# Finding the tokens of an expert's tile: scattered rows and a sorted table, or a sorted order inverted by one-hot products and gathered rows

## The chip, the core and the metric

One core of one Trainium2 chip runs the kernel. The metric is the device time of one execution in microseconds. Engines: TensorE (PE), VectorE (DVE), ScalarE (ACT), GpSimd (POOL), SyncE (SP); 16 transfer engines move data between the core's SBUF and HBM. PSUM holds what TensorE writes.

## The reference

`x` is 4 x 1024 tokens of 256 numbers, normalised per token to `xn`. The result is the sum of three things:

```python
xn = _layernorm(x, axis=-1)
x = x + attention(xn, Wq, Wk, Wv) + experts(xn, w_gate, w_in, w_out)

# experts: 8 experts, each token goes to its two best
logits = xt @ w_gate.T
top_logits, top_idx = jax.lax.top_k(logits, 2)
gates = (one_hot(top_idx, 8) * softmax(top_logits)[..., None]).sum(axis=1)
for e in range(8):
    y = y + gates[:, e:e+1] * ((xt @ w_in[e].T) @ w_out[e].T)
```

The attention has 16 heads by 4 batches, 64 independent problems of 1024 positions with 16 features each (the heads are cut out of the projections by a plain reshape), followed by a normalisation over each batch.

## The kernel before

The tokens are taken as 32 tiles of 128 (`NT`), in 8 chunks of 4 tiles (`NC`, `TC`).

**Products and projections** (to about 224 us). For each expert, `w_in` and `w_out` are multiplied into one 256 x 256 matrix (`mm`). VectorE and GpSimd normalise each chunk into `xn`. TensorE transposes a chunk (`transposes`, L1006), projects values and gate logits (`project_v`, L1033: four groups of six products a chunk) and queries and keys (`project_qk`, L1018: four outputs of six products). ScalarE reads each output of `project_qk` out of PSUM (L580), VectorE subtracts to get the low half (L710), SyncE stores both (L336). Outputs 2 and 3 wait until outputs 0 and 1 have been read by both, since two PSUM banks are shared.

**The plan of the sorted order**, on VectorE, for each half of the tokens (`PARTS` = 2, 16 tiles each): `choose_experts` and `count_choices` every second chunk; TensorE's `rank_choices` turns counts into ranks; `start_tiles` finds how many tiles of 128 rows each expert gets and where they start; `place_choices` gives each token and choice its row number `placeu` in the sorted order (row 128 * tile + row in tile); `place_padding` finds rows for the ends of tiles; `name_owners` (L805 to L812) packs the expert of each of the 40 tiles (`TILES`) into words that TensorE reads. For part 0 this stands in chunk 4, for part 1 after chunk 7.

**The sorted table.** When a part is placed, GpSimd issues 32 indirect transfers (L462), each of which scatters one tile's 128 rows of `xn` to their places in the DRAM table `xs_d`, once for each choice, and then 8 more (L468) that write zero rows into the padding.

**The experts** (about 284 to 381 us). 80 sorted tiles are worked in 20 blocks of 4. SyncE's `sorted_tokens` (L390) loads a block from `xs_d` into one of two halves of `xnc`; TensorE transposes it, ScalarE and VectorE split it into `xth` and `xtl`, `expert_tile` (L1117) multiplies each tile by its expert's matrix, ScalarE and VectorE add the halves, and SyncE's `expert_rows` (L394) stores the block to `ys_d`. From block 4 on, each block also carries one step of attention maxima (`max_scores`, `maxima`). The four output buffers are used in turn, so ScalarE waits at block 4 for the store of block 0.

**The attention loop** (from about 381 us) goes over 64 heads by batches, two ahead with the maxima. In every second round GpSimd gathers a token tile's two expert rows from `ys_d` (L480, two indirect transfers) and weighs and adds them.

SyncE's queue is in order. Its part around the change, after the last stores of `project_qk`: `regroup` 0 to 7 (L323), the loads `features` of the first four rounds (L355) after a wait for `att_const` >= 2, `values(0)` (L360), and only then the expert blocks. `att_const` counts the constant fills of `kf` (GpSimd, L450, ones) and `ot`. The queue's lines around the first block:

```python
for n in range(SLOTS):
    sp.wait_ge(regrouped[n % BC], 16 * (n // BC + 1))
    features(n)
sp.wait_ge(v_stored, 16 * NC)
values(0)
...
sp.wait_ge(m_ready, KT * E)
sorted_tokens(0)
sorted_tokens(1)
```

## Time and profile before

| | us |
|---|---|
| median of three runs | 1091.26 |
| lowest, highest | 1086.12, 1094.1 |
| the profiled execution, its own time | 1090.37 |
| its span, first to last instruction | 1087.7 |

| engine | busy in the span |
|---|---|
| TensorE | 85% |
| VectorE | 75% |
| ScalarE | 62% |
| GpSimd | 26% |

A row of a timeline reads: start in us, duration in us, engine, line of the kernel, instruction, what it writes <- what it reads, count, and in brackets how long the engine stood idle before it and what ended that. PE rows show when products start; their ends are modelled. A row of the chain of waits is a start, a duration and what held the end back at that time; "issue" is time in which nothing was waited for that the profile shows. For an indirect transfer the duration is GpSimd's own work, not the movement of data.

### The profile page before, as it was taken

The page shows a single profiled execution, that of the slowest core. Times are in us where ns is not written, and L with a number is a line of the kernel's source. Part 1 is how long each engine was busy: PE and PEld are TensorE (multiplying, and loading weights), DVE is VectorE, ACT ScalarE, POOL GpSimd, SP SyncE. Part 2 cuts the span into 40 slices and gives each one's busy share as a digit, 9 for nine tenths or more (in the row PEclk, how much of TensorE's full clock was granted, in tenths as well). Part 3 has the DMA queues.
Part 4 walks back from the last instruction along what each step waited for, and adds up shares of the span by engine and source line. Part 5 has one row for each costly group of instructions (what it writes and reads, how often), then busy time and mean ns, then how long its engine had stood idle before and what let it go on. Part 6 is the DMA issues. An engine that isn't in the chain of part 4 may idle for free.

```text
span 1087.7 us, 20730 instructions
## 1 busy us (share of the span) xinstructions
PE 926.8 (85%) x7540; PEld 464.2 (43%) x7540; DVE 821.0 (75%) x1106; ACT 678.4 (62%) x1347; POOL 283.5 (26%) x450
## 2 busy tenths in 40 slices
PE   7886852520499999999999999999999999999994
PEld 6765741520387733333333333333333333333332
DVE  4452540350188779999999999999999999989976
ACT  2210420210165568888888888888888888878884
POOL 2000057127400013232222223232323232223230
PEclk9997986665599979999999999999999999999998
DMA  8675475376587524333333433343334333333214
GB/s 290 236 278 194 149 221 158 112 228 199 159 265 231 175 70 112 100 100 98 105 101 97 103 103 103 93 110 100 103 90 112 100 98 100 105 98 90 73 45 155
DMA packets 155075, 148.44 MB, mean 136 GB/s; under 512 B 84064, under 2 KB 125792, under 8 KB 154976
## 3 DMA queue, kind: packets, MB, share of 16 engines
q1 hardware_dynamic: 148064, 128.24, 40.0%
q0 software_dynamic: 6912, 18.88, 5.6%
q8 instruction: 61, 1.00, 0.4%
q14 instruction: 38, 0.31, 0.1%
HBM read 99.62 MB, written 63.18 MB: 150 GB/s over the span
## 4 chain that ended last, share of the span: by engine, by line
PE 69%; DMA 13%; SPq 5%; issue 4%; DVE 3%; another core or an unknown queue 3%; ACT 2%; POOL 0%; ACTq 0%; POOLq 0%; DVEq 0%
PE ps L1166 21%; PE ps L1148 19%; DMA qf<-ot 10%; PE ps L1136 8%; PE ps L1117 6%; PE ps L1045 5%; PE ps L1018 3%; PE ps L1006 2%; PE ps L1033 2%; SPq L355 2%; DMA wp<-w_out_t 1%; SPq L370 1%; PE ps L1189 1%; DMA xnc<-xs_d 1%
## 5 line engine op out<-in xcount | busy, mean ns | idle before, releaser
L826 DVE TENSOR_REDUCE negm<-ps 128x1 f32<-128x1024 f32 x512 | 619.9, 1223 | 42.4 <-PE ps L1136 22.9
L630 ACT ACTIVATE wp<-ps 128x512 f32<-128x512 f32 x684 | 369.8, 602 | 64.2 <-PE ps L1148 44.3
L1148 PE MATMUL ps<-qf,kf 50*128 50x512 f32 x1024 | 390.3, 456 | 9.1 <-DMA qf<-ot 7.1
L1136 PE MATMUL ps<-kf,qf 48*128 48x512 f32 x1024 | 365.9, 449 | 0.8 <-DVE negm L826 0.7
L1148 PEld LDWEIGHTS ps<-qf,kf 50*128 50x128 f32 x1024 | 162.1, 186 | 216.1 <-ACT wp L630 99.7
L1166 PE MATMUL ps<-wp,vb 128*17 128x256 f32 x2736 | 215.8, 387 | 0.1
L1136 PEld LDWEIGHTS ps<-kf,qf 48*128 48x128 f32 x1024 | 146.9, 186 | 6.0 <-issue 5.0
L630 ACT ACTIVATE vstage<-ps 128x512 f32<-128x512 f32 x170 | 102.3, 602 | 31.5 <-PE ps L1148 21.2
L501 POOL TENSOR_TENSOR mpart<-negm,zero 128x8 fp32r<-128x8 f32 x64 | 13.1, 205 | 397.0 <-DVE negm L826 397.0
L630 ACT ACTIVATE picks<-ps 128x512 f32<-128x512 f32 x170 | 102.4, 602 | 0.0
L1166 PEld LDWEIGHTS ps<-wp,vb 128*17 128x17 f32 x2736 | 46.9, 95 | 116.7 <-issue 40.5
L462 POOL DMA_INDIRECT xs_d<-xn,placeu x64 | 62.3, 973 | 90.9 <-DVE placeu L786 72.0
L695 DVE TENSOR_TENSOR xtl<-ps,xth 128x512 fp32r<-128x512 f32 x56 | 36.4, 687 | 63.7 <-issue 53.0
L555 ACT CAST xth<-ps 128x512 fp32r<-128x512 f32 x56 | 30.5, 590 | 66.4 <-issue 56.9
L508 POOL TENSOR_TENSOR xn<-xn,odd 128x256 f32<-128x256 f32 x32 | 23.5, 733 | 172.7 <-DVE odd L843 172.7
L1006 PE MATMUL ps<-ident,xnc 128*128 128x128 f32 x160 | 23.3, 294 | 52.5 <-issue 52.5
L480 POOL DMA_INDIRECT xnc<-ys_d,placeu x64 | 62.1, 971 | 15.5 <-issue 10.5
L1117 PE MATMUL ps<-mm,xth 128*128 x160 | 61.9, 433 | 4.6 <-issue 4.5
L1045 PE MATMUL ps<-wp 128*128 128x256 f32 x176 | 45.9, 422 | 19.9 <-DMA wp<-w_out_t 18.9
L710 DVE TENSOR_TENSOR spare<-ps,stage 128x512 f32<-128x512 f32 x20 | 13.8, 692 | 58.0 <-issue 30.1
L1166 PE MATMUL ps<-vstage,vb 128*17 128x256 f32 x680 | 53.6, 387 | 0.2 <-issue 0.2
L1166 PE MATMUL ps<-picks,vb 128*17 128x256 f32 x680 | 53.2, 385 | 0.0
(171 smaller groups left out, 895.2 us busy)
## 6 DMA issues: line engine op xcount, KB each, us to landing
feat_d<-qk_d SPq DMA_DIRECT2D x64, 256.0 KB, 3.5
qf<-feat_d SPq DMA_DIRECT2D x128, 128.0 KB
xnc<-xs_d SPq DMA_DIRECT2D x20, 512.0 KB
qf<-feat_d SPq DMA_DIRECT2D x128, 64.0 KB
kf<-feat_d SPq DMA_DIRECT2D x128, 64.0 KB
qk_d<-wp SPq DMA_DIRECT2D x24, 256.0 KB
wp<-w_in SPq DMA_DIRECT2D x11, 512.0 KB, 5.1
wp<-w_out_t SPq DMA_DIRECT2D x11, 512.0 KB, 6.5
```

Source lines behind the costliest of these rows:

```text
L462: nc.gpsimd.indirect_dma_start(out=xs_d[part], out_offset=bass.IndirectOffsetOnAxis(ap=placeu[:, k, t:t + 1], axis=0), in_=xn[:, t, :], in ...
L480: nc.gpsimd.indirect_dma_start(out=xnc[:, t % 2, k, :], out_offset=None, in_=ys_d[part], in_offset=bass.IndirectOffsetOnAxis(ap=placeu[:, ...
L630: nc.scalar.activation(weight_tile(n, j, b)[:, h * HALF:(h + 1) * HALF], ps[:, ST_BANK[(2 * unit + b) % 3], :], ACT.Exp).then_inc(exp_done, 1)
L695: nc.vector.tensor_tensor(xtl[:, p, kt, :], ps[:, XT_BANK[kt], :], xth[:, p, kt, :].bitcast(FP32), ALU.subtract).then_inc(xtl_done, 1)
L826: nc.vector.tensor_reduce(negm[:, n % 2, qt:qt + 1], ps[:, b:b + 2, :].rearrange("p b c -> p (b c)"), AX.X, ALU.max, negate=True).then_inc ...
L1006: last = nc.tensor.transpose(ps[:, XT_BANK[kt], t * P:(t + 1) * P], tokens[:, kt * P:(kt + 1) * P], ident[:])
L1018: last = nc.tensor.matmul(ps[:, PROJECT_BANK[o % 2], :], w[:, o // 2, kt, (o % 2) * P:(o % 2 + 1) * P], v[:, p, kt, :], start=i == 0, stop ...
L1045: last = nc.tensor.matmul(ps[:, M_BANK[dh], 0:D], win[slot][:, h, dh * P:(dh + 1) * P], wout[slot][:, h, :], start=s == 0 and h == 0, stop ...
L1117: last = nc.tensor.matmul(ps[:, Y_BANK[i % 4], 0:columns], v[:, p, kt, tokens], m[:, kt, bass.ds(e * (2 * D), columns)], start=j == 0, sto ...
L1136: last = nc.tensor.matmul(ps[:, max_bank(turn) + half, :], qf[rows, u, qt * P:(qt + 1) * P], kf[rows, u, :], start=True, stop=True)
L1148: nc.tensor.matmul(ps[:, ST_BANK[(2 * unit + half) % 3], :], kf[rows, u, j * P:(j + 1) * P], qf[rows, u, h * HALF:(h + 1) * HALF], start=T ...
L1166: last = nc.tensor.matmul(ps[32 * c:32 * c + VW, PV_BANK, 0:POS // 4], vb[:, n % 2, j + b * NKT // 2, :], weight_tile(n, j, b)[:, c * (POS ...
```

## The change

The sorted table and the scatters go. SyncE stores the normalised tokens plainly into `xn_d` (`tokens_out`, one store of 0.5 MB a chunk: four ahead of the stores of chunk 2, then one behind the stores of each of chunks 2 to 5). VectorE and TensorE invert the sorted order: for each of a part's 32 pairs of token tile and choice, `row_hot` holds a one where the row number in the tile equals the column, `tile_hot` the token's number where the tile equals the column, and 32 products added up in one PSUM bank give, for each row of each of the 40 tiles, which token belongs there; padding rows give token 0. `take_sources` copies that to `source`. GpSimd then gathers each sorted tile from `xn_d` straight into `xnc`, 80 gathers in all, and from the third block on waits until TensorE has transposed the block that was in the buffer. The one-hots lie in `qf` and `kf`, so `kf` is filled with ones only afterwards, by VectorE; SyncE's `features` wait for that. `place_padding` goes. In part 0, `find_sources` stands at the head of chunk 5 and `take_sources` at the head of chunk 6; on TensorE the 32 products stand between the transposes of chunk 6 and `project_qk` of chunk 5.

```diff
+            def tokens_out(c):
+                part, first = c * PARTS // NC, c * CH % (PT * P)
+                sp.wait_ge(xn_done, TC * (c + 1))
+                sp.dma_start(xn_d[part][first:first + CH].rearrange("(t p) d -> p t d", p=P), xn[:, TC * c:TC * (c + 1), :]
+                             ).then_inc(xn_out[part], 16)
...
+            for c in range(NC // PARTS):
+                tokens_out(c)
             for c in range(2, NC):
                 values_out(c)
                 qk_halves_out(c)
+                if c + 2 < NC:
+                    tokens_out(c + 2)
...
-            sp.wait_ge(m_ready, KT * E)
-            sorted_tokens(0)
-            sorted_tokens(1)
             for b in range(NMB):
-                if b + 2 < NMB:
-                    sorted_tokens(b + 2)
...
-            nc.gpsimd.memset(kf[:].bitcast(FP32), 1.0).then_inc(att_const, 1)
...
-            for part in range(PARTS):
-                for k in range(2):
-                    pool.wait_ge(placed, 2 * part + k + 1)
-                    for t in range(PT * part, PT * (part + 1)):
-                        nc.gpsimd.indirect_dma_start(
-                            out=xs_d[part], out_offset=bass.IndirectOffsetOnAxis(ap=placeu[:, k, t:t + 1], axis=0),
-                            in_=xn[:, t, :], in_offset=None).then_inc(scattered[part], 16)
-                pool.wait_ge(att_const, 2)
-                pool.wait_ge(padded, part + 1)
-                for e in range(E):
-                    nc.gpsimd.indirect_dma_start(
...
+            for part in range(PARTS):
+                pool.wait_ge(sourced, part + 1)
+                pool.wait_ge(named, part + 1)
+                pool.wait_ge(xn_out[part], 16 * NC // PARTS)
+                for i in range(TILES):
+                    b = part * MB + i // TC
+                    if i % TC == 0 and b >= 2:
+                        pool.wait_ge(xt_psum, KT * (NC + b - 1))
+                    nc.gpsimd.indirect_dma_start(
+                        out=xnc[:, b % 2, i % TC, :], out_offset=None, in_=xn_d[part],
+                        in_offset=bass.IndirectOffsetOnAxis(ap=source[:, part, i:i + 1], axis=0)).then_inc(xs_in[b % 2], 16)
+                    if b == WARM + NKT + 3 and i % TC == TC - 1:
+                        max_halves(0)
...
+            def find_sources(part):
+                count, tiles, base, place, placef, owner, packed, work, row, tile, split = plans[part]
+                rows = slice(PT * part, PT * (part + 1))
+                parts = split.bitcast(mybir.dt.uint32).rearrange("p (h k t) -> p h k t", h=2, k=2)
+                for half, (op, number, out) in enumerate(((ALU.bitwise_and, P - 1, row), (ALU.logical_shift_right, 7, tile))):
+                    g(nc.vector.tensor_scalar(parts[:, half], placeu[:, :, rows], number, None, op))
+                    g(nc.vector.tensor_copy(out, parts[:, half].rearrange("p k t -> p (k t)")))
+                g(nc.vector.tensor_tensor(tile_hot, iota[:, 0:TILES].unsqueeze(1).to_broadcast([P, 2 * PT, TILES]),
+                                          tile.unsqueeze(2).to_broadcast([P, 2 * PT, TILES]), ALU.is_equal))
+                for k in range(2):
+                    own = tile_hot[:, k * PT:(k + 1) * PT]
+                    g(nc.vector.tensor_tensor(own, own.bitcast(FP32), token[:].unsqueeze(2).to_broadcast([P, PT, TILES]), ALU.mult))
+                for k in range(2):
+                    own = slice(k * PT, (k + 1) * PT)
+                    nc.vector.tensor_tensor(row_hot[:, own], iota[:].unsqueeze(1).to_broadcast([P, PT, P]),
+                                            row[:, own].unsqueeze(2).to_broadcast([P, PT, P]), ALU.is_equal).then_inc(hot, 1)
+                dve.wait_ge(hot, 2 * (part + 1))
+
+            def take_sources(part):
+                dve.wait_ge(found, part + 1)
+                nc.vector.tensor_copy(source[:, part], ps[:, RANK_BANK[part], 0:TILES]).then_inc(sourced, 1)
...
-            place_padding(1)
+            find_sources(1)
             name_owners(1)
+            take_sources(1)
+            nc.vector.memset(kf[:].bitcast(FP32), 1.0).then_inc(att_const, 1)
...
+            def find_sources(part):
+                for k in range(2):
+                    pe.wait_ge(hot, 2 * part + k + 1)
+                    for t in range(k * PT, (k + 1) * PT):
+                        last = nc.tensor.matmul(ps[:, RANK_BANK[part], 0:TILES], row_hot[:, t].bitcast(FP32),
+                                                tile_hot[:, t].bitcast(FP32), start=t == 0, stop=t == 2 * PT - 1)
+                last.then_inc(found, 1)
```

## Rows read from the trace of the kernel before

**Rows 1.** Busy time by stage: stretch, its length, busy us of each engine, clock, DMA, GB/s.
```profile
150.00:202.00 52.00, 10.86 (x33) 7.13 (x31) 4.13 (x8) 4.30 (x10) 33.70 (x35) 0.63 0.54 161
202.00:224.10 22.10, 21.04 (x98) 17.27 (x98) 10.74 (x34) 8.49 (x24) 0.00 (x0) 0.87 0.50 162
224.10:284.30 60.20, 1.66 (x7) 1.40 (x7) 12.23 (x59) 0.79 (x2) 36.78 (x38) 0.53 0.69 210
284.30:380.60 96.30, 89.99 (x513) 73.48 (x513) 72.86 (x135) 51.00 (x119) 2.33 (x4) 0.92 0.66 207
380.60:1060.00 679.40, 669.18 (x6175) 258.51 (x6175) 629.77 (x599) 562.73 (x1068) 188.99 (x317) 0.99 0.36 96
```

**Rows 2.** Timeline of ScalarE, chunk 5: it reads outputs of `project_qk`.
```profile
172.43 0.59 ACT L580 CAST stage<-ps 128x512 fp32r<-128x512 f32 x1 [9.51 <-remote]
189.42 0.59 ACT L580 CAST stage<-ps 128x512 fp32r<-128x512 f32 x1 [16.41 <-issue]
200.90 0.59 ACT L580 CAST stage<-ps 128x512 fp32r<-128x512 f32 x1 [10.89 <-remote]
```

**Rows 3.** Timeline of TensorE, chunk 5: first and last products of the third output.
```profile
163.79 1.22 PE L1018 MATMUL ps<-xth,wqkh 128*128 128x512 f32 x2 [9.26 <-issue]
...
165.67 1.05 PE L1018 MATMUL ps<-xth,wqkl 128*128 128x512 f32 x2
```

**Rows 4.** Timeline of GpSimd: a fill; first and last transfers of part 0; last of part 1.
```profile
3.03 1.80 POOL L450 MEMSET kf<- 128x2048 f32 x1
...
143.41 1.25 POOL L462 DMA_INDIRECT xs_d<-xn,placeu  x1 [30.18 <-DVE placeu L786]
...
193.32 0.96 POOL L468 DMA_INDIRECT xs_d<-ot,padu  x1 [0.31 <-issue]
...
285.73 0.96 POOL L468 DMA_INDIRECT xs_d<-ot,padu  x1 [0.30 <-issue]
```

**Rows 5.** Chain of waits, from the first feature load to the first expert transposes.
```profile
243.69 1.15 SPq L355
...
270.09 12.71 DMA xnc<-xs_d
...
284.29 1.94 PE ps L1006 x8
```

**Rows 6.** Chain of waits in the projections and in the experts.
```profile
149.40 0.87 PE ps L1006 x8
...
202.26 4.33 PE ps L1033 x18
...
221.03 3.08 PE ps L1018 x12
...
308.49 0.87 PE ps L1006 x8
...
374.19 0.87 PE ps L1006 x8
```

**Rows 7.** Timeline of VectorE: end of part 0's planning; part 1's last placing, padding, first owner step.
```profile
150.05 0.17 DVE L812 CAST words<-xnc 128x5 int32<-128x5 f32 x1
...
236.50 0.17 DVE L786 TENSOR_SCALAR placeu<-wp 128x16 uint32<-128x16 f32 x1
...
238.25 0.23 DVE L799 TENSOR_SCALAR padu<-wp,lane 128x8 uint32<-128x8 f32 x1
238.52 0.45 DVE L805 TENSOR_TENSOR wp<-iota,wp 128x280 f32<-128x280 f32 x1
```

**Rows 8.** Timelines: ScalarE with and without a gather pair just before; GpSimd's last gather.
```profile
497.40 0.60 ACT L630 ACTIVATE vstage<-ps 128x512 f32<-128x512 f32 x1 [0.33 <-PE ps L1148]
...
506.29 0.60 ACT L630 ACTIVATE vstage<-ps 128x512 f32<-128x512 f32 x1 [0.23 <-PE ps L1148]
...
1054.31 0.95 POOL L480 DMA_INDIRECT xnc<-ys_d,placeu  x1 [0.30 <-issue]
1057.12 1.04 POOL L487 TENSOR_TENSOR xnc<-xnc,gates 128x512 f32<-128x512 f32 x1 [1.86 <-DMA xnc<-ys_d,placeu]
```

More of the change, by code:

```diff
@@ L62, in attention_and_experts @@
     v_d = nc.dram_tensor("v_d", [T, 2, NKT * VW], FP32, kind="Internal").ap()
-    xs_d = [nc.dram_tensor(f"xs_d{i}", [TILES * P, D], FP32, kind="Internal").ap() for i in range(PARTS)]
+    xn_d = [nc.dram_tensor(f"xn_d{i}", [PT * P, D], FP32, kind="Internal").ap() for i in range(PARTS)]
     ys_d = [nc.dram_tensor(f"ys_d{i}", [TILES * P, D], FP32, kind="Internal").ap() for i in range(PARTS)]
@@ L118, in attention_and_experts @@
         before = sb("before", [P, PT + 1, E])
-        padu = sb("padu", [P, PARTS, E], mybir.dt.uint32)
+        source = sb("source", [P, PARTS, TILES], mybir.dt.uint32)
         placeu = sb("placeu", [P, 2, NT], mybir.dt.uint32)
         words = sb("words", [P, PARTS, WORDS], mybir.dt.int32)
-        odd = sb("odd", [P, D])
+        odd = lg[:].rearrange("p t e -> p (t e)")
         wp = sb("wp", [P, 4, POS])
@@ L208, in attention_and_experts @@
         placed = sem("placed")
-        padded = sem("padded")
+        hot = sem("hot")
+        sourced = sem("sourced")
+        found = sem("found")
         named = sem("named")
-        scattered = sem("scattered", PARTS)
+        xn_out = sem("xn_out", PARTS)
         xs_in = sem("xs_in", 2)
@@ L759, in start_tiles @@
             def start_tiles(part):
-                count, tiles, base, place, placef, owner, packed, work, filled, excess, inside = plans[part]
+                count, tiles, base, place, placef, owner, packed, work, row, tile, split = plans[part]
                 bank = RANK_BANK[part]
@@ L770, in start_tiles @@
                                           iota[:, 0:MOST].unsqueeze(1).to_broadcast([P, E, MOST]), ALU.is_gt))
-                g(nc.vector.reduce_sum(tiles[:, :, 0], more, AX.X))
-                g(nc.vector.tensor_tensor(tiles[:, :, 1], tiles[:, :, 0], count, ALU.subtract))
-                g(nc.vector.memset(base[:, 0], 0.0))
-                for e in range(E):
-                    g(nc.vector.tensor_tensor(base[:, e + 1], base[:, e], tiles[:, e], ALU.add))
+                g(nc.vector.reduce_sum(tiles, more, AX.X))
+                g(nc.vector.memset(base[:, 0:1], 0.0))
+                for e in range(1, E):
+                    g(nc.vector.tensor_tensor(base[:, e:e + 1], base[:, e - 1:e], tiles[:, e - 1:e], ALU.add))
                 g(nc.vector.tensor_tensor(place, ps[:, bank, 0:PT * E].rearrange("p (t e) -> p t e", e=E),
-                                          base[:, 0:E, 0].unsqueeze(1).to_broadcast([P, PT, E]), ALU.add))
+                                          base.unsqueeze(1).to_broadcast([P, PT, E]), ALU.add))
             def place_choices(part):
-                count, tiles, base, place, placef, owner, packed, work, filled, excess, inside = plans[part]
+                count, tiles, base, place, placef, owner, packed, work, row, tile, split = plans[part]
                 rows = slice(PT * part, PT * (part + 1))
@@ L787, in place_choices @@
                     dve.wait_ge(placed, 2 * part + k + 1)
[L789 to L800 removed]
+            def find_sources(part):
+                count, tiles, base, place, placef, owner, packed, work, row, tile, split = plans[part]
+                rows = slice(PT * part, PT * (part + 1))
[13 more added lines that the diff above has]
+                dve.wait_ge(hot, 2 * (part + 1))
@@ L802, in name_owners @@
+            def take_sources(part):
+                dve.wait_ge(found, part + 1)
+                nc.vector.tensor_copy(source[:, part], ps[:, RANK_BANK[part], 0:TILES]).then_inc(sourced, 1)
             def name_owners(part):
-                count, tiles, base, place, placef, owner, packed, work, filled, excess, inside = plans[part]
+                count, tiles, base, place, placef, owner, packed, work, row, tile, split = plans[part]
                 past = work[:, 0:TILES * (E - 1)].rearrange("p (i e) -> p i e", e=E - 1)
-                g(nc.vector.tensor_tensor(past, iota[:].unsqueeze(2).to_broadcast([P, TILES, E - 1]),
-                                          base[:, 1:E, 0].unsqueeze(1).to_broadcast([P, TILES, E - 1]), ALU.is_ge))
+                g(nc.vector.tensor_tensor(past, iota[:, 0:TILES].unsqueeze(2).to_broadcast([P, TILES, E - 1]),
+                                          base[:, 1:E].unsqueeze(1).to_broadcast([P, TILES, E - 1]), ALU.is_ge))
@@ L884, in _ @@
                 planned = c == NC // PARTS
+                if c == NC // PARTS + 1:
+                    find_sources(0)
+                if c == NC // PARTS + 2:
+                    take_sources(0)
                 if c % PAIR == 0 and c > PAIR:
@@ L1096, in _ @@
                     rank_choices(0)
+                if c == NC // PARTS + 1:
+                    find_sources(0)
                 for o in range(4):
@@ L1099, in _ @@
             rank_choices(1)
+            find_sources(1)
             def owner_words(part):
```

51 lines of the change are left out of this document (16 added, 35 removed).

## Prediction

> **What bounds the kernel now.** I read four views in this order: the busy time by stage, the chain of waits, the timelines of each engine where the chain breaks off, and the groups of operations for prices. By stage [rows 1], 679 of 1087.7 us are the attention loop (from 380.6), in which TensorE, VectorE and ScalarE are all nearly full. The change leaves that loop alone, so whatever it gives or takes lies before 380.6. There two stages are nearly empty: from 150 to 202 TensorE is busy 10.9 of 52 us, and from 224.1 to 284.3 it is busy 1.7 of 60 us. VectorE and ScalarE are empty there as well, while GpSimd issues indirect transfers in both.
>
> The second gap is plain in the chain [rows 5]. SyncE issues the loads of the attention features from 243.7 on. Only after them, at 270.1, comes the load of the first sorted block. It lands 12.7 us later, and TensorE starts on the experts at 284.3. Even a faster load could not help much: the last of the scatters that must land before the first load of part 1, and that share the transfer engines, is issued at 285.7 [rows 4].
>
> The first gap is odd. ScalarE reads the second, third and fourth result of `project_qk` of chunk 5 at 172.4, 189.4 and 200.9 [rows 2], after waits of 9.5, 16.4 and 10.9 us. TensorE's six products that the read at 189.4 takes are shown from 163.8 to 166.7 [rows 3]. Nothing else stands between. So a result of TensorE reaches its reader some 20 us late. This begins about 6 us after the first scatter is issued and ends at 200.9; GpSimd issues the 40 scatters of part 0 from 143.4 to 194.3 [rows 4]. Afterwards the same work flows: the last three value groups of chunk 6 start at 202.3, and all is done at 224.1 [rows 6]. I read the gap as the price of the scatter stream. From 149.4 to 202.3 TensorE gets through one set of transposes (0.9), four outputs of `project_qk` (two take 3.1, so 6.2) and one value group (about 1.0) [rows 6]: 8.1 us of work in 52.9. The rest, 44.8 us over 40 scatters, is 1.12 us for each.
>
> **What the change removes.** All 80 scatters (two parts of 32 and 8), the 20 sorted loads from SyncE's queue, eight padding steps per part on VectorE (1.8 us, from the end of the placing to that of the padding [rows 7]), and two small steps of planning (0.4). The constant fill of `kf` leaves GpSimd (1.8 [rows 4]) where it was hidden.
>
> **What it adds, stage by stage.**
>
> *Chunk 5.* `find_sources(0)` stands at the head of chunk 5 on VectorE, ahead of all that TensorE waits for. Steps of 16 and 280 elements take 0.17 and 0.45 [rows 7], so 1.06 ns for each further element. Four small steps cost 0.7, the tile one-hot of 1280 elements 1.5, two products of 640 together 1.7, two row one-hots of 2048 2 x 2.32 = 4.6, and nine gaps of 0.03 0.3: 8.8 us. VectorE ended its planning at 150.2 [rows 7]; without padding it ends at 148.4, and with the new work at 157.2. TensorE then has 16 of its 32 small products left. A transpose with the same 128-column weight costs 0.109 at the 2.4 GHz clock (granted 1.0) and 0.243 at 1.2 GHz [rows 5, 6], so 1.7 to 3.9; I take 2.8. Chunk 5's `project_qk` starts at 160.0 and takes 6.2. Chunks 6 and 7 take 22.8, from 201.3 (202.3 less the first value group) to 224.1. TensorE ends the projections at 189.0, before at 224.1. The new stores of 0.5 MB a chunk lie beside it: the transfer engines were at half load from 202 to 224 [rows 1]. If they did bind, four chunks of 0.52 MB at the full rate (162 GB/s at half load, so 324) would be 6.5 us. I take nothing.
>
> *Between projections and experts.* In the old kernel the second placing ended at 236.7 [rows 7], 12.6 after 224.1; 12.2 without the two steps. Add 8.8 for `find_sources(1)`, 3.9 for the last 16 products at the low clock of this stretch (0.53 [rows 1]), 0.2 for `take_sources`, 1.8 for the fill of `kf`, bounded by GpSimd's row. `name_owners` hides under the products. Sum 26.9, where the old kernel took 60.2. The fill holds up `features` on SyncE, and behind them `values(0)` and `expert_rows`. Features and values took 26 us [rows 5], so the first block's rows leave at about S + 26, S being the start of the experts. ScalarE needs that slot again only at block 4, at S + 24 by the old pace (308.5 less 284.3 [rows 5, 6]). I take nothing; it could be some 5 us, once.
>
> *Experts.* Blocks 0 and 1 are fetched long before. The other 18 need 72 gathers at 1.28 each (39 steps from 143.4 to 193.3 [rows 4]): 92.2. GpSimd may start on block 2 once the first transposes are done (1.9), the last block lands 1.9 after its issue (1055.3 to 1057.1 [rows 8]), and from the last transposes at 374.2 to the end it is 6.4 [rows 1, 6]. The chain by GpSimd is 102.4, TensorE's own 96.3 [rows 1], hence 6.1 slower.
>
> *The unknown.* What does a gather cost TensorE? I call it s. 8 gathers lie in the projections and 72 in the experts, so the experts end at the later of 318.3 + 8s (GpSimd) and 189.0 + 26.9 + 96.3 + 80s = 312.2 + 80s (TensorE). The upper bound is the scatter's 1.12. The lower is 0, a transfer that takes nothing from TensorE; that it would help is excluded. In between lies the one mark that I find, a wait of ScalarE for TensorE of 0.33 in the step after the pair, 0.23 in the like step without gathers [rows 8]. The nearest row is the gather's own, though it shows pairs and no stream. I put the whole 0.33 on a pair, s = 0.17. Then the experts end at 325.8 instead of 380.6, 54.8 earlier. The span becomes 1032.9, and with the 2.7 around it **1036 us**. The profiled run (1090.4) is 0.9 below the median of three, which changes nothing here.
>
> The Trainium skill speaks against my reading of the first gap. "SBUF — State Buffer", section "Who interferes with whom", says that the DMA side and the engine side are disjoint and that "PE and ACT never wait on anyone". By it the late results are not the scatters' doing. This case's rows show the coincidence and not the mechanism, so it is carried as a rival.
>
> **The rivals.**
>
> *A stream of gathers costs like a stream of scatters* (s = 1.12). For it: both come from the same queue at the same pace, and a pair may be too short to build up what 40 in a row did. Against it: the old kernel's first eight transposes for the experts, at 284.3, show 1.9 us, the plain low-clock time, although 78 scatters had been issued by then [rows 4, 5]. Experts' end 312.2 + 89.6 = 401.8, time 1112. The gain is gone from s = 0.86 on. Chance 0.17, of which 0.02 within 1%.
>
> *In between* (s from 0.3 to 0.85): 1046 to 1090, middle 1066. Chance 0.20, 0.03 of it within 1%.
>
> *The late results have another cause and stay.* The projections then end at 224.1 + 9.8 (planning until 160.0 instead of 150.2) = 233.9, the experts at 233.9 + 26.9 + 102.4 = 363.2, time 1073. That is the time by the skill's sentence above. Against it speaks that the standstill begins and ends with the scatters. Chance 0.10.
>
> *Faster still*, below 1020, if GpSimd gets ahead or the small products cost less: 0.05.
>
> **How the numbers follow.** The likeliest case (s below 0.3, 1028 to 1046) has 0.48, and 1036 is its value at s = 0.17; with the stores binding it would reach 1052. The range must take in the middle and the third rival, so 1020 to 1090. Outside are 0.05 below and 0.15 above. A measurement of this kernel tells about 1% from no change. Faster by more: 0.48 + 0.17 + 0.10 + 0.05 = 0.80. Within 1%: 0.05. Slower: 0.15.
>
> **What would show it.** Chunk 5's four reads by ScalarE about 1.5 us apart, and the projections' end near 190: the first gap was the scatters'. VectorE's six large steps together 7.7, TensorE's 32 small products within 8. First expert transposes near 217. Then GpSimd without pause at 1.28 a gather, and blocks of experts about 5.1 us apart. If the blocks are 6 or more apart, with TensorE's results read late, the rivals with the larger s are right. If GpSimd waits for transposes between blocks, the landing time is what I have too small. The attention loop should keep its 679 us; a change there I have not foreseen.

## The result and the profile after

The changed kernel takes 1073.3 us (median of 4 runs) against 1091.7 for the kernel before on the same chip: a ratio of 0.984, 95% interval 0.980 to 0.988. On another chip, in a later group of runs, it was 0.989 (0.985 to 0.994). The forecast was 1036. So the change makes the kernel faster, by 1.6% and a third of what I expected. The profiled execution took 1073.4 us with a span of 1071.4, beside the forecast span of 1032.9: 38.5 us are missing.

Busy time by stretch, changed kernel: the rest of the projections, the gap to the experts, the experts, and all that follows. Columns: stretch, its length, busy time of TensorE, its weight loads, VectorE, ScalarE and GpSimd with instructions, granted clock, share of the transfer engines, GB/s.

```profile
145.00:202.50 57.50, 45.68 (x225) 38.63 (x224) 25.61 (x59) 14.30 (x42) 7.81 (x8) 0.85 0.54 179
202.50:237.50 35.00, 15.54 (x71) 15.13 (x71) 20.67 (x60) 0.79 (x2) 0.00 (x0) 0.57 0.48 128
237.50:374.80 137.30, 102.43 (x513) 80.76 (x513) 74.34 (x138) 49.54 (x120) 68.47 (x74) 0.84 0.57 160
374.80:1071.40 696.60, 681.71 (x6311) 262.16 (x6311) 646.01 (x626) 577.36 (x1092) 191.04 (x320) 0.98 0.37 100
```

The same two last stretches of the kernel before, cut at the same marks (first expert transposes, first attention product):

```profile
284.30:382.10 97.80, 90.44 (x513) 73.63 (x514) 73.92 (x138) 51.37 (x120) 2.33 (x4) 0.92 0.65 204
382.10:1087.70 705.60, 682.79 (x6311) 264.42 (x6311) 646.22 (x626) 576.36 (x1092) 191.69 (x320) 0.98 0.37 99
```

Both gaps of [rows 1] have shrunk, as forecast: the projections end at 202.5 us instead of 224.1, and the experts start 35 us later instead of 60. But the expert stage takes 137.3 us instead of 97.8, 39.5 more. I had allowed it some 14 more. And the attention loop with its tail, which the change does not touch, is 9.0 us shorter.

Timeline of ScalarE, changed kernel, the four reads of chunk 5's `project_qk`; and later waits for TensorE in chunk 6, then one for a store:

```profile
170.33 0.59 ACT L579 CAST stage<-ps 128x512 fp32r<-128x512 f32 x1 [15.89 <-PE ps L1030]
171.65 0.59 ACT L579 CAST stage<-ps 128x512 fp32r<-128x512 f32 x1 [0.73 <-PE ps L1030]
173.49 0.58 ACT L579 CAST stage<-ps 128x512 fp32r<-128x512 f32 x1 [1.25 <-PE ps L1030]
174.89 0.59 ACT L579 CAST stage<-ps 128x512 fp32r<-128x512 f32 x1 [0.81 <-PE ps L1030]
...
185.87 0.58 ACT L579 CAST wp<-ps 128x512 fp32r<-128x512 f32 x1 [2.52 <-remote]
188.72 1.07 ACT L579 CAST wp<-ps 128x512 fp32r<-128x512 f32 x2 [2.27 <-remote]
194.14 0.17 ACT L563 COPY lg<-ps 128x8 f32<-128x8 f32 x1 [4.34 <-DMA v_d<-vstage]
```

("remote" is a wait whose end the profile can't put to any instruction.) The reads that waited 9.5, 16.4 and 10.9 us in [rows 2] now wait 1.3 us at most. What delays them is the 15.9 us ahead of the first: the planning. The chain of waits shows how that time is made up, for part 0 and then part 1, with the store that binds in between:

```profile
149.36 1.50 DVE kf L794
150.89 0.84 DVE kf L798
...
152.61 2.30 DVE qf L801
154.96 12.66 PE ps L1105 x64
...
181.78 12.29 DMA v_d<-vstage
...
218.78 2.30 DVE qf L801
221.12 13.89 PE ps L1105 x64
```

VectorE's steps have the sizes that I gave them (1.50, 0.84, 2.30). The 32 small products do not: they are 64 records, in 12.7 us.

In the experts three kinds of waits appear. GpSimd's timeline at the head of blocks; ScalarE's; one start of TensorE's transposes; and two pieces of the chain of waits:

```profile
252.18 0.94 POOL L504 DMA_INDIRECT xnc<-xn_d,source  x1 [2.54 <-PE ps L1018]
...
258.40 0.94 POOL L504 DMA_INDIRECT xnc<-xn_d,source  x1 [1.54 <-PE ps L1018]
...
284.49 0.94 POOL L504 DMA_INDIRECT xnc<-xn_d,source  x1 [9.49 <-PE ps L1018]
```

```profile
251.71 0.92 ACT L610 COPY spare<-ps 128x256 f32<-128x256 f32 x3 [2.51 <-remote]
...
278.35 0.37 ACT L610 COPY spare<-ps 128x256 f32<-128x256 f32 x1 [10.95 <-DMA ys_d<-spare]
...
300.50 0.37 ACT L610 COPY stage<-ps 128x256 f32<-128x256 f32 x1 [3.18 <-remote]
```

```profile
268.94 1.10 PE L1018 MATMUL ps<-ident,xnc 128*128 128x128 f32 x8 [1.25 <-DMA xnc<-xn_d,source]
```

```profile
262.23 16.10 DMA ys_d<-spare
...
294.24 5.53 DMA xnc<-xn_d,source
```

GpSimd is not the unbroken chain that I assumed. It waits 1.1 to 4.5 us for TensorE's transposes at 12 of the 18 blocks that it gathers in the stage, and 9.5 us at one more; between the long waits a block takes about 6 us instead of 5.1. ScalarE waits 2.5 to 3.2 us for some results: the products that the read at 300.50 takes had ended at 297.7. At block 4 everything stands for some 10 us, until the first expert rows, whose store is issued at 262.23, have landed in `ys_d` at 278.33. And the gathers land later than the 1.9 us of the forecast: the block whose transposes start at 268.94 had its last gather issued at 262.15, 6.8 us before, and the chain has another with 5.5. With two buffers, GpSimd gets through without a wait only if the block has landed and is transposed within about 6.2 us of its last issue (five gathers of 1.25), so a landing time like this alone makes it wait.

### The profile page after: what moved, and what is told of

Same layout as the page of the kernel before. It is cut to its first block, busy times and chain, and to the rows that moved or that the text cites. A ratio compares the mean times of both kernels' runs of the same rounds, so it can differ in the third digit from the quotient of the medians.

```text
span 1071.4 us, 20973 instructions
## 1 busy us (share of the span) xinstructions
PE 960.4 (90%) x7668; PEld 493.0 (46%) x7668; DVE 836.1 (78%) x1107; ACT 677.3 (63%) x1347; POOL 279.2 (26%) x448
## 3 DMA queue, kind: packets, MB, share of 16 engines
q1 hardware_dynamic: 141728, 121.95, 38.5%
## 4 chain that ended last, share of the span: by engine, by line
PE 73%; DMA 9%; DVE 6%; SPq 5%; issue 3%; ACT 1%; POOL 1%; POOLq 0%; ACTq 0%; DVEq 0%
PE ps L1189 25%; PE ps L1171 21%; PE ps L1159 10%; PE ps L1057 4%; DMA qf<-ot 3%; PE ps L1030 2%; PE ps L1140 2%; DMA v_d<-vstage 2%; PE ps L1105 2%; SPq L364 2%; SPq L345 2%; DMA ys_d<-spare 2%; PE ps L1018 1%; DMA wp<-w_out_t 1%; PE ps L1200 1%
## 5 line engine op out<-in xcount | busy, mean ns | idle before, releaser
L504 POOL DMA_INDIRECT xnc<-xn_d,source x80 | 75.9, 948 | 169.4 <-PE ps L1018 82.7
L629 ACT ACTIVATE vstage<-ps 128x512 f32<-128x512 f32 x170 | 102.4, 602 | 27.6 <-PE ps L1171 16.5
L1140 PE MATMUL ps<-mm,xth 128*128 x160 | 67.6, 463 | 21.1 <-DVE spare L824 13.3
L492 POOL TENSOR_TENSOR xn<-xn,lg 128x256 f32<-128x256 f32 x32 | 23.4, 731 | 172.7 <-DVE lg L850 172.6
L694 DVE TENSOR_TENSOR xtl<-ps,xth 128x512 fp32r<-128x512 f32 x56 | 37.1, 687 | 19.4 <-ACT xth L554 12.7
L1057 PEld LDWEIGHTS ps<-wp 128*128 128x128 f32 x176 | 37.2, 215 | 26.6 <-issue 11.3
L641 ACT COPY ot<-ps 128x384 f32<-128x384 f32 (+1 forms) x64 | 30.4, 476 | 22.5 <-PE ps L1212 20.5
```

The lines of the kernel that those rows point to most:

```text
L504: nc.gpsimd.indirect_dma_start(out=xnc[:, b % 2, i % TC, :], out_offset=None, in_=xn_d[part], in_offset=bass.IndirectOffsetOnAxis(ap=sourc ...
L629: nc.scalar.activation(weight_tile(n, j, b)[:, h * HALF:(h + 1) * HALF], ps[:, ST_BANK[(2 * unit + b) % 3], :], ACT.Exp).then_inc(exp_done, 1)
L641: nc.scalar.copy(ot[:, 0:groups, n % 2, :], ps[:, PV_BANK, 0:groups * TB].rearrange("p (g t) -> p g t", t=TB)).then_inc(pv_evac, 1)
L694: nc.vector.tensor_tensor(xtl[:, p, kt, :], ps[:, XT_BANK[kt], :], xth[:, p, kt, :].bitcast(FP32), ALU.subtract).then_inc(xtl_done, 1)
L1057: last = nc.tensor.matmul(ps[:, M_BANK[dh], 0:D], win[slot][:, h, dh * P:(dh + 1) * P], wout[slot][:, h, :], start=s == 0 and h == 0, stop ...
L1140: last = nc.tensor.matmul(ps[:, Y_BANK[i % 4], 0:columns], v[:, p, kt, tokens], m[:, kt, bass.ds(e * (2 * D), columns)], start=j == 0, sto ...
```

## The experiments

All ratios are to the kernel before on the same chip. A run is called by the first part of its label (e5, b3). "Stage" is the expert stage, from its first transposes to the first attention product.

**The small products.** The changed kernel with

```diff
-  nc.tensor.matmul(..., row_hot[:, t].bitcast(FP32), tile_hot[:, t].bitcast(FP32), ...)
+  nc.tensor.matmul(..., row_hot[:, t], tile_hot[:, t], ...)
```

> The changed kernel with the 64 small products that find the source tokens read as FP32R instead of FP32, nothing else. In the changed kernel they are 64 records in 12.7 us at 155 us and 64 records in 13.9 us at 221 us, two for each product of about 0.2 us. Theory A (the two passes of an FP32 product are what my estimate left out, and both places lie on the path that sets the end): 32 records of 0.2 us, 6.3 and 7 us less, the span 11 to 13 us shorter. Theory B (chunk 5's end is set by the stores that the vstage buffer waits for, so the first place gives nothing): 7 us less, all of it between 215 and 237 us. Theory C (the one-hots' weight loads or VectorE's one-hots are the bound): no change.

Chain of waits of this kernel, the same two places:

```profile
156.09 2.30 DVE qf L801
158.43 7.01 PE ps L1105 x32
...
217.76 7.03 PE ps L1105 x32
```

32 records in 7.0 us at both places, 5.7 and 6.9 less. The time is 1063.6 us, ratio 0.976 (0.969 to 0.982). The products gave what theory A says. The projections ended only 3.4 us earlier (199.7 by the end of their last read, for 203.1), since the products of part 0 also started 3.5 us later in this execution (158.4 for 155.0, behind VectorE's one-hots); in part 1 nothing took the gain away. One product is 0.22 us in FP32R and 0.40 in FP32, both at a granted clock of 0.50 to 0.55. In the forecast I had priced it by a transpose (0.109 to 0.243), which is FP32 too but is recorded once.

**The features ahead of the stores.** The changed kernel with SyncE's list reordered:

```diff
-  for n in range(SLOTS): features(n)
-  values(0)
   for b in range(NMB):
+      if b < SLOTS: features(b)
+      if b == SLOTS: values(0)
       if b: expert_rows(b - 1)
```

> The changed kernel with SyncE's list changed: the four feature blocks and the first values are issued one at a time between the first stores of expert outputs, instead of all ahead of the first store. Theory A (the stall at the expert stage's block 4, 9.5 us of GpSimd's and 10.9 us of ScalarE's waiting for ys_d<-spare, comes from the store behind the features on SyncE): the stall is gone, the expert stage 139 us becomes 128 to 131, the time 8 to 11 us shorter. Theory B (the store itself is slow because the DMA engines are full with the features' transfers, 16.1 us for 0.5 MB, and would be in any order): under 3 us.

ScalarE has no wait for `ys_d` left in the stage, and the stage takes 130.0 us, 7.4 less. The time is 1066.4, ratio 0.978 (0.971 to 0.986). So the stall at block 4 was the queue, as theory A has it. The prediction had named it ("some 5 us, once") and put it at nothing. For e1 and e2 alike the gain is read from the stretches: the intervals of their ratios overlap that of the changed kernel (0.980 to 0.988), so that the whole times don't show it by themselves.

**No gathers.** The changed kernel with 20 plain loads in place of the 80 gathers:

```diff
-  nc.gpsimd.indirect_dma_start(out=xnc[:, b % 2, i % TC, :], in_=xn_d[part], in_offset=source...)
+  sp.dma_start(xnc[:, b % 2], xn_d[b // MB][first:first + CH]...)
```

> The changed kernel with the 80 gathers of the expert stage replaced by 20 plain loads of the same bytes from the same table, issued by SyncE two blocks ahead as in the kernel before; the search for the sources stays, its result is not used, so that the rows reach the experts unsorted (this part of the computation is left out). Theory A (the gathers make the stage 139 us instead of 96: GpSimd's pace, their latency and TensorE's late results while they are generated): the stage takes 97 to 108 us, the time 30 to 40 us shorter, and no ScalarE read waits over 1.5 us for a TensorE result in it. Theory B (features and stores in the DMA queues are what lengthened it): 120 us or more.

1054.8 us, ratio 0.965 (0.959 to 0.972), and a stage of 116.9 us, 20.4 less than the changed kernel's: between the two theories. The chain of waits tells why:

```profile
255.76 12.98 DMA xnc<-xn_d
268.78 1.97 PE ps L1026 x8
...
282.83 2.09 PE ps L1148 x12
...
300.04 2.11 PE ps L1148 x12
```

The load of block 2 stands behind the features on SyncE and costs about 20 us at the start. Afterwards a block takes 4.3 us (from 282.83 to 300.04 are four), and no read of ScalarE is late. TensorE's own pace is thus 4.3 us, and the changed kernel's 6 are the gathers' doing (late results and late landings together; this run takes both away). The store and feature traffic is a second, separate cause, which shows as soon as the first is gone.

**What the scatters did.** The kernel before with part 0's 40 scatters held back:

```diff
   for part in range(PARTS):
       for k in range(2):
-          pool.wait_ge(placed, 2 * part + k + 1)
+          pool.wait_ge(placed, 2 * PARTS)
```

> The kernel before, with the 40 scatters of part 0 held back until part 1 is placed, so that none is issued during chunk 5 of the projections; all is still computed. Theory A (the stream of scatters made TensorE's results late, 1.12 us each over 40): chunk 5 has no ScalarE read that waits over 2 us, the projections end at 196 to 202 us instead of 224; afterwards 80 scatters in a row take 102 us from about 197, so that the experts start 15 to 35 us later relative to the projections' end and get late results themselves: the time 1090 to 1130. Theory B (the late results have another cause, such as the stores of q and k halves): the projections still end at 218 or later.

The projections end at 186.5 us instead of 224.7 (last read ended), the chunk-5 reads follow each other as in the changed kernel. The standstill has moved to where the scatters now are, from 198.8 to 300 us. Timeline of ScalarE there:

```profile
275.49 0.58 ACT L555 CAST xth<-ps 128x512 fp32r<-128x512 f32 x1 [10.80 <-remote]
286.63 0.58 ACT L555 CAST xth<-ps 128x512 fp32r<-128x512 f32 x1 [10.56 <-remote]
297.83 0.37 ACT L611 COPY spare<-ps 128x256 f32<-128x256 f32 x1 [10.61 <-remote]
```

One result comes through every 11 us, which is about nine scatters. The time is 1107.5, ratio 1.012. Whoever moves the scatters moves the standstill with them: that they cause it is shown. 38.2 us over 40 scatters are 0.96 us each, stores that they slow included (see e8 below); my reading of [rows 2 to 4] had 1.12.

**Scatter or gather, bytes or count, stream or single.** Three variants of the kernel before. The first pauses the stream, the other two keep the real scatters back as above and put 32 small transfers (128 rows of 128 bytes) in their place:

```diff
+  if part == 0 and t % 4 == 3:
+      pool.wait_ge(scattered[part], 16 * (k * PT + t + 1))
```

```diff
+  nc.gpsimd.indirect_dma_start(out=<idle xnc>, in_=x as rows of 32, in_offset=placeu...)      # e6
+  nc.gpsimd.indirect_dma_start(out=small_d, out_offset=placeu..., in_=xn[:, t, 0:32])         # e7
```

> The kernel before, with GpSimd waiting, after every fourth token scatter of part 0, until those already issued have landed; all is computed. With the scatters held back until later chunk 5 had no late result and the projections ended at 186.5 us instead of 224.7. Theory A (what delays TensorE's results is an unbroken run of indirect transfers, and a pause lets them through): the reads of chunk 5 wait at most 5 to 6 us each (four scatters) instead of 8.3 to 15, the projections end at 195 to 205 us, the time 0 to 25 us shorter (the stream takes eight waits of some 2 us longer). Theory B (each scatter costs TensorE its 1.12 us, paused or not): the projections still end at 220 or later.

> The kernel before with part 0's 40 scatters held back until part 1 is placed, as in e4_late_scatters, and in their old place, from 149 us, 32 gathers of 128 rows of 128 bytes each (from the input into an idle buffer; extra work, the rest is all computed). Theory A (any unbroken run of indirect transfers holds TensorE's results, gathers too): reads of chunk 5 wait 8 us and more, the projections end at 210 to 225 instead of 186.5. Theory B (only scatters do it): the projections end at 186 to 190.

> As e6_small_gathers, with 32 scatters of 128 rows of 128 bytes (into a table of their own) in place of the 32 gathers. Theory A (it is the generating of the transfers, not their 1 KB rows, that holds TensorE's results): the projections end at 210 to 225, as with 1 KB rows. Theory B (bytes in the DMA engines or in SBUF's read path): 186 to 195.

And one to see whether the place of the buffers changes the attention loop, with `odd = lg[:]...` as in the changed kernel:

> The kernel before with the attention rows of a pair kept in the idle logits buffer instead of a buffer of their own, as the changed kernel does; this moves every buffer behind it by 1 KB per partition. The 29 rounds of the attention loop took 622.5 and 623.8 us in the two kernels with the old buffers and 614.5 to 616.9 in the four with the new ones, the difference in waits for the maxima's rows (qf<-ot). Theory A (it comes from where the buffers lie): 614 to 618 us, the time 6 to 9 us shorter. Theory B (it comes from the phase in which the loop is entered, or from the tables in HBM): 621 to 625 us, the time the same within 3 us.

None of these four says what it was sent to say. e5 ended its projections at 197.6 us, e6 at 194.6, e7 at 194.3; but e8, which issues exactly the old 40 scatters in a row, ended them at 206.6, and its reads are not late at all. Timeline of ScalarE in e8:

```profile
155.90 0.59 ACT L580 CAST stage<-ps 128x512 fp32r<-128x512 f32 x1 [1.26 <-PE ps L1018]
157.31 0.59 ACT L580 CAST stage<-ps 128x512 fp32r<-128x512 f32 x1 [0.82 <-PE ps L1018]
171.49 0.17 ACT L564 COPY lg<-ps 128x8 f32<-128x8 f32 x1 [13.60 <-DMA v_d<-vstage]
```

In this group the scatters only slow a store (13.6 us of waiting for `v_d`). TensorE's results are in time. The kernel before was itself faster here, 1080.2 us against 1093.1 in the first group. Either the chip of this group did not show the effect, or the moved buffers took it away (e8 has them; in e5 to e7 the scatters were paused or replaced). The ratios were 0.989 (0.985 to 0.993) for e5 and 0.998 (0.995 to 1.002) for e8; e6 and e7 ran once each, at 1072.8 and 1071.9 us.

The same three kernels went to another chip, beside a profile of the kernel before and of the changed one on a third:

> The kernel before, unchanged, profiled on the chip of this group. In the second group of runs no kernel showed a late TensorE result, though one of them (e8_att_in_lg) issued the same 40 scatters in a row; in the first group and in the two profiles shown at the start they came up to 24 us late. Theory A (the delay belongs to some chips and not to others): either late results as in the first profile (projections' end 220 to 228 us) or none (204 to 210), and the other three kernels of this group alike. Theory B (it was the 1 KB shift of the buffers in e8_att_in_lg and the held-back scatters in the others that took it away): projections' end 220 to 228 us here on any chip.

> The changed kernel, unchanged, on the same chip. Theory A: if the kernel before shows no late results here, neither does this one, and the expert stage is 8 to 12 us shorter than the 137 us of its first profile, the stall at block 4 kept; the ratio to the kernel before stays between 0.975 and 0.99. If it shows them, the profile is as the first.

> The same kernel as e8_att_in_lg, on another chip. Theory A (late TensorE results belong to some chips; three groups showed them, one did not): with late results the projections end at 218 to 228 us, without them at 204 to 208, and the three kernels beside it agree. Theory B (the 1 KB shift of the buffers took them away): 204 to 208 here though the others of the group show them.

> The same kernel as e6_small_gathers: the kernel before with part 0's scatters held back and 32 gathers of 128 rows of 128 bytes from 149 us on. If this chip shows late results at all: Theory A (any unbroken run of indirect transfers holds TensorE's results, gathers as scatters): reads of chunk 5 that wait 4 to 16 us, the projections' end at 205 to 222. Theory B (gathers do far less): 186 to 197.

> The same kernel as e5_scatter_pauses: a wait for landing after every fourth scatter of part 0. If this chip shows late results at all: Theory A (a pause lets them through): no read of chunk 5 waits over 6 us, the projections end at 190 to 205. Theory B (each transfer costs its 1.12 us, paused or not): 218 or later.

The kernel before again ended its projections at 223.6 us with reads that waited up to 15.8 us, the changed one is as in its first profile (stage 136.7). The buffers are acquitted: e14, the same program as e8, ended at 225.9. Timeline of ScalarE in e14, then in e13 (small gathers):

```profile
170.28 0.59 ACT L580 CAST stage<-ps 128x512 fp32r<-128x512 f32 x1 [8.61 <-issue]
186.69 0.59 ACT L580 CAST stage<-ps 128x512 fp32r<-128x512 f32 x1 [15.82 <-issue]
200.18 0.59 ACT L580 CAST stage<-ps 128x512 fp32r<-128x512 f32 x1 [12.91 <-remote]
```

```profile
157.99 0.17 ACT L571 COPY lg<-ps 128x8 f32<-128x8 f32 x1 [8.20 <-remote]
167.13 0.59 ACT L562 CAST xth<-ps 128x512 fp32r<-128x512 f32 x1 [8.70 <-issue]
178.28 0.59 ACT L562 CAST xth<-ps 128x512 fp32r<-128x512 f32 x1 [10.56 <-issue]
```

Gathers hold TensorE's results as scatters do. Their projections end at 215.3 us, 28.8 later than e4's without any stream; over 32 gathers that is 0.90 us each, beside 0.96 for a scatter. Their rows are an eighth of the size, so it is not the bytes. These prices hold two things. The same two programs without late results, e8 and e6, ended at 206.6 and 194.6, which is still 20.1 and 8.1 later than e4, through stores to `v_d`. The late results themselves are the rest: 19.3 us for the 40 scatters (e14 less e8) and 20.7 for the 32 small gathers (e13 less e6).

e12, which pauses after every fourth scatter, ended at 198.2 on this same chip, and none of its chunk-5 reads waits over 1.3 us. Its part 1 goes out without pauses, from 252 us on, and there results come late again in the same execution. Timeline of ScalarE in e12:

```profile
157.68 0.59 ACT L582 CAST stage<-ps 128x512 fp32r<-128x512 f32 x1 [1.26 <-PE ps L1020]
...
289.01 0.58 ACT L557 CAST xth<-ps 128x512 fp32r<-128x512 f32 x1 [10.89 <-remote]
300.16 0.58 ACT L557 CAST xth<-ps 128x512 fp32r<-128x512 f32 x1 [10.56 <-remote]
```

So what holds the results is an unbroken run, not each transfer, as far as one execution tells; the pauses also halve the rate (part 0's 40 transfers take 107 us instead of 51), and these two were not taken apart. Pausing was no gain for the whole kernel: part 1's stream then overlapped the experts, and e12 took 1109.3 us, beside 1090.3 for the kernel before on that chip (e14 1088.8, e13 1134.0, one run each).

Whether the groups differ by their chip or by something else of the machine I can't say. The chip numbers of the runs speak against a fixed trait of a chip: the group of e15 and e16 below has the same chip number as that of e12 to e14, and the kernel before took 1078.4 us in it for 1090.3. e7 was not repeated, so for small scatters it stands open whether they hold results.

**A version that gathers ahead.** Seven token buffers instead of two (three idle attention weight tiles and the projection weights, free after chunk 7):

```diff
-  out=xnc[:, b % 2, i % TC, :]
+  out=ring[b % RING][:, i % TC, :]     # ring = xnc x2, wp[:, 1:4], wqkh, wqkl
-  if b >= 2: pool.wait_ge(xt_psum, KT * (NC + b - 1))
+  if b >= RING: pool.wait_ge(xt_psum, KT * (NC + b - RING + 1))
```

> The changed kernel with seven token buffers for the expert stage instead of two: the two of before, three of the idle attention weight tiles and the two tiles of the projection weights, idle once chunk 7 is done; so GpSimd gathers blocks 0 to 6 before the stage begins. Theory A (the stage's 137 us come from GpSimd's gathers at 1.25 us waiting for a free buffer and TensorE for them; TensorE's own work is 4.3 us a block, as the run with plain loads showed): stage 90 to 105 us, the time 30 to 45 us shorter. Theory B (the stream of gathers itself, or the features and stores, hold TensorE): stage 120 us or more, the time less than 20 us shorter.

> e9_ring7 with the single-pass products of e1_single_pass and the feature blocks issued in turn with the stores as in e2_feature_turns. If the three add: 10 us from the products, and 5 to 8 us from the stores' stall beyond e9_ring7, the span near 1015 us. If the stall was a consequence of the late gathers, only the 10 us are added.

e9 takes 1067.7 us, ratio 0.983 (0.979 to 0.986), 7.5 us less than the changed kernel on this chip. Its stage takes 121.8, 15 less, and not the 90 to 105 of theory A. So the waits of GpSimd for a buffer were a part of the cost and not the larger one. e10, with the single-pass products and the feature order, takes 1044.7 us, **ratio 0.961 (0.956 to 0.966)**, stage 121.0. It beats both kernels. Busy time by stretch, e10, while gathers run (all but the last block's four, which stand at 307.5 to 311.3), and after:

```profile
221.40:305.00 83.60, 65.78 (x313) 52.32 (x313) 42.24 (x80) 30.34 (x74) 49.12 (x52) 0.79 0.69 189
305.00:342.40 37.40, 33.86 (x202) 26.94 (x202) 31.42 (x60) 19.44 (x47) 4.22 (x6) 1.00 0.44 128
```

From 305 us on 202 records of products take 37.4 us. Before it, 313 take 83.6, where the same pace would give 58. The granted clock is 0.79 there and 1.00 after, so that TensorE's own busy time grows as well.

**Pauses in the better version, and no gathers in it.**

> e10_all with GpSimd waiting, after the four gathers of each block, until they have landed. e10_all lost some 35 us in its expert stage (121 us against 20 blocks of 4.3) while the gathers ran, to 305 us, and none after. Theory A (pauses let TensorE's results through): 100 to 108 us for the stage, bound at first by TensorE and then by GpSimd at 7 us a block, the time 8 to 18 us shorter than e10_all, near 1030. Theory B (each gather costs its share): the stage 120 us or more, the time 1044 or longer.

> e10_all with the 80 gathers replaced by 20 plain loads of the same bytes, issued by SyncE into the same seven buffers (the rows reach the experts unsorted: this part of the computation is left out). Theory A (the stream of gathers costs e10_all's stage some 30 us): the stage takes 86 to 97 us, the span 1010 to 1020 us. Theory B (the features, the stores and the attention scores' share of VectorE do it): 110 us or more.

> e10_all with GpSimd waiting for landing after every second block (8 gathers), and its first maxima split three blocks earlier, so that TensorE does not wait for them as it did for 26 us in e11_all_pauses. GpSimd's pace is then 6 to 7.5 us a block, 14 blocks from 225 us: a stage of 100 to 110 us and a time 8 to 18 us below e10_all (0.945 to 0.955 of the kernel before) if the pauses let TensorE's results through and the features do not stretch the waits; a stage of 125 us or more and a time above 1045 us if the waits for landing grow as in e11_all_pauses (4 to 7 us each).

e11 decides nothing between its theories: each wait for landing took GpSimd 2 to 8 us, and it became the bound. Its stage took 153.2 us, 26 of them for the split maxima that GpSimd came to late. The time was 1076.2, ratio 0.985 (0.977 to 0.993).

e15, without any gather, was to have a stage near 90 and has 113.6. ScalarE waits for stores, three times:

```profile
259.80 0.37 ACT L628 COPY spare<-ps 128x256 f32<-128x256 f32 x1 [8.23 <-DMA ys_d<-spare]
269.04 0.37 ACT L628 COPY spare<-ps 128x256 f32<-128x256 f32 x1 [7.06 <-DMA ys_d<-spare]
278.10 0.37 ACT L628 COPY stage<-ps 128x256 f32<-128x256 f32 x1 [6.88 <-DMA ys_d<-stage]
```

These are 22.2 us; without them the stage would be 91.4. Theory A missed, since the second cause took the first one's place: as soon as TensorE is quick, its four output buffers run out while SyncE still feeds features. e16 takes 1040.4 us, ratio 0.965 (0.960 to 0.971), stage 116.9 and not the 100 to 110 expected, with the same store waits (8.7 and 10.2 us). e15, which has no gather, took 1040.9 in its one run: with all 80 gathers e16's stage is only 3.3 us longer, and its whole time no longer (e15 loads through SyncE's queue instead and splits its first maxima later, so the 3.3 are not the gathers' price alone). In this group the kernel before took 1078.4, and ScalarE's waits for products in e16 are those of e15 within 0.2 us (2.9, 2.1, 2.7 and 3.9). That is how the group without late results looked (1080.2 there, 1088 to 1093 in the others), so e16 does not show that its pauses help.

## Why the prediction was wrong

**The first gap.** Right in its cause, and now shown (e4 and e12). My four reads "about 1.5 us apart" came. The projections' end is 13.5 us later than forecast (202.5 for 189.0). Of it 7.6 are the small products: the last one ends at 167.6 instead of 160.0. I had left them 2.8 us after the second one-hot, at the price of a transpose. The rest, some 6, lies in chunks 6 and 7: two reads that wait 2.5 and 2.3 us while the eight gathers run, and 4.3 us for a store to `v_d`. I had bounded the stores at 6.5 and taken nothing.

**Projections to experts.** 35.0 for 26.9, and 7.7 of the 8.1 are the products again (they end at 235.0, 11.6 after the second one-hot, where I had 3.9). So the step "a transpose with the same 128-column weight costs 0.109 ... and 0.243 ..., I take 2.8" failed as a price, and is worth 15.3 us: a product was two records and 0.40 us. Read as FP32R (e1) the 0.22 would have been near the 0.243.

**The experts.** Forecast, to the mark used here, 215.9 to 327.3 (the 325.8 of the sum and the 1.5 that the first attention product stands behind it in [rows 1] and the row 382.10 above): 111.4. Measured 137.3, 25.9 more. The step that failed is "I put the whole 0.33 on a pair, s = 0.17". It read the price of a stream from pairs. In an unbroken stream a gather costs 0.90 us (e13), five times that; the pair of [rows 8] shows 0.1, and the stage lies in between, since GpSimd's run is broken at most blocks. Put wholly on the gathers, the measured end of the experts gives s = 0.49 (373.3 less the 21.6 of the two earlier stretches is 351.7; less 312.2, over 80).

A second term of the same sum failed with it, "the last block lands 1.9 after its issue", read from a pair too. In the stage gathers took 5.5 and 6.8 us to land, and GpSimd waited for transposes: the sign that the prediction had named for a landing time taken too small, beside blocks 6 us apart for a larger s. Both came. A third is "the first block's rows leave at about S + 26 ... I take nothing". The store did leave then (262.2, S + 24.7), but ScalarE needs its landing, and that came 16.1 us later; e2 gave 7.4 of some 10 us back. The granted clock is 0.84 (0.92 before), and TensorE's own busy time in the stage grows from 90.4 to 102.4. These parts overlap, and the runs don't split the 25.9 between them: e9, e15 and e16 show that none, taken away alone, gives its full size.

So the rival "in between" (1046 to 1090, middle 1066) names a right mechanism, a gather's price between a pair's and a stream's, but that the measured time lies in it is partly luck: it counts neither the 15.3 us of products nor the stall, nor the 9.0 that the loop gave back. The rival s = 1.12 has nearly the right price for a stream, but no stream like that is in the changed kernel.

**The loop.** Not foreseen: 9.0 us shorter, and 5.0 in the pair of profiles of the third group (698.7 for 703.7). It isn't chance. From the first attention product of round 1 to that of round 30, the ten kernels built on the old one took 619.8 to 623.8 us, the ten built on the new one 613.4 to 616.9, whatever happened ahead of it. The waits of the products of queries and keys for the maxima's rows (`qf<-ot`) are shorter, but by less than the loop gains:

```profile
L1148 PE MATMUL ps<-qf,kf 50*128 50x512 f32 x1024 | 391.1, 457 | 6.5 <-DMA qf<-ot 4.1 <-issue 1.1 <-DVE negm L826 0.7
```

```profile
L1171 PE MATMUL ps<-qf,kf 50*128 50x512 f32 x1024 | 391.7, 458 | 3.8 <-DMA qf<-ot 2.3 <-issue 1.1
```

(this line's products in the kernel before, then in the changed one, third group of runs; busy us, mean ns, then idle time and its releasers). The place of the attention rows is not it: e8 and e14 took 620.7 and 620.5. What else of the change does it stays open.

Together: 13.5 + 8.1 + 25.9 - 9.0 = 38.5 us.

**The rival from the skill.** The Trainium skill, "SBUF — State Buffer", section "Who interferes with whom", has "PE and ACT never wait on anyone". I had carried it as a rival at 1073, which by accident is the measured time. Its mechanism is not there: the standstill went with the scatters in e4. The sentence stands in a section on the SBUF ports and can still hold for execution, since TensorE's products ran when they were due [rows 3]; what comes late is their completion at the reader. The other way is prompt: VectorE's subtraction of the first result ended at 163.74, and TensorE started at 163.79.

## What to carry to other kernels

Price a new operation by a row of the same kind in the same setting: a stream of transfers not by a pair (its landing time neither), an FP32 product not by a transpose, a store not by when it leaves but by when it lands. Before costing a moved step at nothing because "it binds only once", write down what will bind when the neighbour gets faster. And profile the unchanged kernel in every group of runs, since an effect of 20 us may be absent in one.

## What the runs showed of the hardware

- An unbroken run of indirect transfers on GpSimd (one each 1.25 to 1.28 us) holds back TensorE's results from ScalarE: waits of up to 16 us, one result in about 11 us (before, e4, e13, e14). With the stores that it slows, a scatter of 1 KB rows costs 0.96 us and a gather of 128 byte rows 0.90. With a wait for landing after every four, no result came late (e12, one execution).
- In one of the groups of runs it did not happen with the same programs (e6 and e8 against e13 and e14). There the 40 scatters still put off the projections' end by 20 us, through stores.
- An FP32 product of 128 by 128 weights and 40 columns is recorded twice and takes 0.40 us, in FP32R once and 0.22, at a granted clock near 0.5 (after, e1).
- Beside feature loads and stores, gathers landed 5.5 and 6.8 us after their issue, where a single pair took 1.9 [rows 8].
